# Deformable convolutions: one image's offsets, distances and tents prepared two images ahead, and the tap images' steps set at other places of three engine programs

## The reference, cut to what matters

```
om = conv3x3(xn, w_off) + b_off            # 27 maps: dy, dx of 9 taps, 9 masks
py, px = base + dy, base + dx ; mask = sigmoid(om[18:27])
sampled[k] = bilinear(xn at py[k], px[k]) * mask[k]      # 9 taps
out = einsum('ckhw,ock->ohw', sampled, w)
```

## Time and profile before

| | us |
|---|---|
| median of 3 runs | 1029.12 (1026.18 to 1031.92) |
| the profiled execution | 1027.65 |
| its span, first to last instruction | 1025.9 |
| convolution 0, first offsets to last result | 19.5 to 153 |
| recurrence | 162 to 597 |
| convolution 1 | 608 to 744 |
| busy: PE, DVE, ACT, POOL | 782.2, 547.0, 557.5, 359.9 |

### The profile page before, as it was taken

How to read it: one execution, slowest core, us unless ns; L and a number is a source line. 1 busy time by engine, 2 the same in 40 slices (tenths; PEclk the granted TensorE clock), 3 DMA queues, 4 the chain that set the end, 5 groups by cost and what they waited for, 6 DMA issues and landing times.

```text
span 1025.9 us, 18107 instructions
## 1 busy us (share of the span) xinstructions
PE 782.2 (76%) x6224; PEld 577.1 (56%) x6224; DVE 547.0 (53%) x1560; ACT 557.5 (54%) x1580; POOL 359.9 (35%) x296
## 2 busy tenths in 40 slices
PE   5789886666666666666666467988859999899996
PEld 2476674555555555555555434767736666466664
DVE  3666753555445445333333335666556667567675
ACT  2565653333345455333333335656548888688884
POOL 0646650000000000000000006475528888588884
PEclk8899995555555555555555558999969999899998
DMA  9500000000001100000000000000000010100000
GB/s 221 149 2 1 2 2 1 1 0 1 1 1 73 73 0 1 1 1 1 1 1 0 1 0 1 2 1 2 2 1 2 1 73 2 75 2 1 2 2 22
DMA packets 5861, 18.54 MB, mean 18 GB/s; under 512 B 1093, under 2 KB 2822, under 8 KB 5254
## 3 DMA queue, kind: packets, MB, share of 16 engines
q1 hardware_dynamic: 5478, 17.21, 5.9%
q10 hardware_dynamic: 288, 0.13, 0.1%
HBM read 9.47 MB, written 0.52 MB: 10 GB/s over the span
## 4 chain that ended last, share of the span: by engine, by line
PE 30%; POOL 20%; DVE 18%; ACT 16%; issue 13%; DVEq 1%; POOLq 1%; DMA 0%; SPq 0%; ACTq 0%
POOL zw L806 20%; PE bank L455 9%; DVE bank L1047 6%; PE bank L457 6%; ACT scan_io L702 5%; ACT tcell L706 4%; PE bank L297 4%; DVE hr L1053 4%; PE bank L332 4%; PE bank L349 3%; DVE hid L881 2%; ACT shi L601 2%; PE bank L319 1%; DVE zw L854 1%; DVE flat L846 1%
## 5 line engine op out<-in xcount | busy, mean ns | idle before, releaser
L766 POOL TENSOR_TENSOR st<-tent,tentx 128x768 f32<-128x768 f32 x96 | 140.6, 1500 | 581.1 <-DVE tentx L874 503.4
L806 POOL TENSOR_TENSOR zw<-hid,zw 128x512 f16<-128x512 f32 x176 | 203.9, 1159 | 49.5 <-ACT zw L733 38.8
L455 PE MATMUL bank<-hr,lv 64*64 64x8 f32 x512 | 96.7, 261 | 158.9 <-DVE hr L1053 158.9
L455 PEld LDWEIGHTS bank<-hr,lv 64*64 64x64 f32 x512 | 72.5, 200 | 205.5 <-DVE hr L1053 205.4
L1152 DVE SCALAR_TENSOR_TENSOR hid<-bank,wsc,st 128x512 f32<-128x512 f32 x176 | 132.0, 751 | 75.8 <-ACT st L737 70.4
L702 ACT ACTIVATE scan_io<-bank 64x16 f32<-64x16 f32 x256 | 49.2, 192 | 210.6 <-PE bank L457 210.4
L495 PE MATMUL bank<-st,wh 128*128 128x512 f16 x352 | 137.0, 389 | 11.7 <-POOL st L799 5.4
L1047 DVE TENSOR_TENSOR_SCAN bank<-scan_io 64x32 f32<-64x32 f32 x256 | 57.6, 225 | 163.1 <-ACT scan_io L702 163.1
L737 ACT ACTIVATE st<-bank,wsc 128x512 f32<-128x512 f32 x176 | 121.0, 687 | 35.2 <-PE bank L496 17.5
L881 DVE SCALAR_TENSOR_TENSOR hid<-bank,shi 128x512 f16<-128x512 f32 x144 | 98.1, 690 | 74.0 <-ACT shi L601 72.7
L496 PE MATMUL bank<-st,wl 128*128 128x512 f16 x352 | 136.6, 388 | 0.0
(11 more groups left out here) (149 smaller groups left out, 1135.8 us busy)
## 6 DMA issues: line engine op xcount, KB each, us to landing
w13s<-w SPq DMA_DIRECT2D x8, 704.0 KB, 16.6
w2f<-w SPq DMA_DIRECT2D x4, 384.0 KB, 26.9
w13s<-wh SPq DMA_DIRECT2D x2, 704.0 KB, 3.4
w13s<-wl SPq DMA_DIRECT2D x2, 704.0 KB, 4.6
wh<-w13s SPq DMA_DIRECT2D x2, 704.0 KB, 3.7
wl<-w13s SPq DMA_DIRECT2D x2, 704.0 KB, 5.2
w2f<-w2p SPq DMA_DIRECT2D x2, 384.0 KB, 5.2
w2p<-w2f SPq DMA_DIRECT2D x2, 384.0 KB, 6.0
```

The costliest lines, as they stand in the source:

```text
L455: nc.tensor.matmul(both[:, 0, t, :], lv[:, C:2 * C], prev, start=False, stop=True, skip_group_check=True)
L766: nc.gpsimd.tensor_tensor(st[p][:, t, k:k + KG, :].rearrange("p k (y x) -> p k y x", x=16), ty, tx, ALU.mult)\
L806: nc.gpsimd.tensor_tensor(hl[:, u % MR, :], hid[:, u % MR, :], hh[:, u % MR, :], ALU.subtract)\
```

## The change: what it does

The chain from offsets to tents (PE `offsets`, `turn_offsets`; ACT `offsets`, `turned`, `tents`, `pads`; DVE `distances`, `weighted`) is done for image m + 2 while image m is worked on, where it was done for m + 1. A second set of these steps, for image 1, moves into the part ahead of the loop. Within the loop, ACT `tents` goes from g = 5 to g = 8 and DVE `weighted` from g = 5 to g = 8. Of the tap images, which stay one image ahead, ACT `taps(m + 1, 0)` goes from g = 6 to g = 5, DVE `tap_images(m + 1, 0)` from g = 6 to g = 4, and PE `taps(m + 1, 1)` from g = 8 to behind the last group. No instruction is added or removed, and no wait's condition changes.

```diff
--- before.py
+++ after.py
@@ -369,18 +369,19 @@
                 turn_offsets(0)
                 pe.wait_ge(s(c + "taps"), 2)
                 taps(0, 0)
+                offsets(1, 0)
+                offsets(1, 1)
+                turn_offsets(1)
                 taps(0, 1)
                 for m in range(B):
                     for g in range(NG):
-                        if m + 1 < B:
+                        if m + 2 < B:
                             if g < 2:
-                                offsets(m + 1, g)
+                                offsets(m + 2, g)
                             elif g == 3:
-                                turn_offsets(m + 1)
-                            elif g == 4:
-                                taps(m + 1, 0)
-                            elif g == 8:
-                                taps(m + 1, 1)
+                                turn_offsets(m + 2)
+                        if g == 4 and m + 1 < B:
+                            taps(m + 1, 0)
                         if g == LAG + 2 and m > 0 and m % 2 == 0:
                             turn(m // 2 - 1)
                         turn_weights(m, g)
@@ -388,6 +389,8 @@
                             sums(m, g - LAG)
                         elif m > 0:
                             sums(m - 1, NG - LAG + g)
+                    if m + 1 < B:
+                        taps(m + 1, 1)
                 for h in range(NG - LAG, NG):
                     sums(B - 1, h)
                 turn(BQ - 1)
@@ -632,25 +635,29 @@
                 turned(0)
                 tents(0)
                 taps(0, 0)
+                offsets(1)
+                turned(1)
                 taps(0, 1)
+                tents(1)
+                pads(2)
                 for m in range(B):
                     for g in range(NG):
                         ended = m // 2 - 1 if m % 2 == 0 and m > 0 else None
-                        if m + 1 < B:
+                        if m + 2 < B:
                             if g == 2:
-                                offsets(m + 1)
+                                offsets(m + 2)
                             elif g == 4:
-                                turned(m + 1)
-                            elif g == 5:
-                                tents(m + 1)
-                            elif g == 6:
-                                taps(m + 1, 0)
+                                turned(m + 2)
+                            elif g == 8:
+                                tents(m + 2)
+                        if g == 5 and m + 1 < B:
+                            taps(m + 1, 0)
                         if g == 4 and ended is not None:
                             summed(ended)
                         if g == 7 and ended is not None:
                             result(ended)
-                        if g == 7 and m + 2 < B:
-                            pads(m + 2)
+                        if g == 6 and m + 3 < B:
+                            pads(m + 3)
                         high(m, g)
                     if m + 1 < B:
                         taps(m + 1, 1)
@@ -889,22 +896,23 @@
                 distances(0)
                 weighted(0)
                 tap_images(0, 0)
+                distances(1)
+                flats(1)
                 tap_images(0, 1)
-                flats(1)
+                weighted(1)
                 for m in range(B):
                     for g in range(NG):
                         low(m, g)
                         if g == 0 and m + 2 < B:
                             flats(m + 2)
-                        if m + 1 < B:
-                            if g == 3:
-                                distances(m + 1)
-                            elif g == 5:
-                                weighted(m + 1)
-                            elif g == 6:
-                                tap_images(m + 1, 0)
-                            elif g == 8:
-                                tap_images(m + 1, 1)
+                        if g == 3 and m + 2 < B:
+                            distances(m + 2)
+                        if g == 4 and m + 1 < B:
+                            tap_images(m + 1, 0)
+                        if g == 8 and m + 2 < B:
+                            weighted(m + 2)
+                        if g == 8 and m + 1 < B:
+                            tap_images(m + 1, 1)
 
             def largest():
 
```

## The result

The changed kernel takes 993.68 us (median of 4 runs, 993.37 to 994.94), the kernel before 1028.9 us (4 runs). The ratio is 0.966, 95% interval 0.9636 to 0.9683: 35 us faster. The direction was right, and so was the wait that the change removes; the cost on VectorE that the forecast took off again was not, and the gain was ten microseconds larger than forecast.

The account below looks back on a forecast made before the run. PE was taken as nearly full, with 24.2 us of tap waits in the loops. Seven images at 91.1 us and starts 2.9 us later gained 12.0 and 13.5 us, giving 1003.5 us, range 996 to 1015.

Parts of the forecast that it names:

- the cost on VectorE: In the loops, VectorE instructions slowed beside GpSimd's products; about 7 us taken off the gain.
- The tap wait: PE's tap matmuls L319 idle for VectorE's L854 in the loops; 24.2 us, to be gone entirely.
- The chain given for it: Late in an image: distances, absolute value, tents, groups, tap copies, L854; tents (0.69 + 0.77 us) stand before the copies.
- The clock: PE's lower clock behind waits in the images would be given back; about 8 us, five images by 1.65.
- I take 0.55 us of new ring wait where there is no `turn`: PE waits for low-part banks in the loops: 0.55 us without turn, 0.2 with; bounds 0 and 1.2 each.
- 12.3: Length of image 5 in us: 11.2 on PE, but set by DVE's 11.6 and its ring.
- The cross-check under the sum: Terms of both signs: 24.2 (waits) + about 8 (clock) - 7 (DVE) = 25 us gained.
- Ahead of the loops: Image 1's added set and the wait for pads(2) make T(0, 0) 2.9 us later in each convolution.
- rival 2: No cost on DVE and a fast start, ring waits zero: 996.5 us; chance 0.10.
- Rival 1: DVE becomes the bound, ring waits of 1.2 us and more in each image: 1014.5 us; chance 0.20.
- rival 3: The wait only changes its place, another of the same length appears: 1027 to 1029 us; chance 0.05.
- rival 4: More short waits leave PE at 1.2 GHz, so slower: 1038 us with 35 us at half clock; chance 0.03.

Follow-up runs that it names:

- experiment 1: The kernel before with only TensorE's taps(m + 1, 1) moved behind the last group: 1007.75 us, ratio 0.980.
- experiment 3: The changed kernel with all tap steps put back where they were, offsets, distances and tents staying two images ahead: 1018.12 us, ratio 0.990.
- experiment 4: The changed kernel with only TensorE's taps(m + 1, 1) put back to g = 8: 993.85 us, ratio 0.968.
- experiment 5: The changed kernel with ScalarE's and VectorE's steps for half 0 of the tap images back at g = 6: 1001.02 us, ratio 0.974.
- experiment 7: The changed kernel with ScalarE's pads(2) and VectorE's flats(1) moved earlier ahead of the loops: 989.14 us, ratio 0.963.
- experiment 2: The kernel before with the tap steps at the changed kernel's places, tents and weighted at g = 6, everything one image ahead: 1001.51 us, ratio 0.975.
- experiment 8: The changed kernel with VectorE's distances done twice for images 2 to 7, first into an unread tile: 1022.76 us, ratio 0.995.
- experiment 6: The changed kernel with VectorE's flats(m + 2) moved from g = 0 to g = 8, ahead of weighted: 994.65 us, ratio 0.969.

## Why the prediction was wrong

**The tap wait: right.** It was put at 24.2 us in the loops and gone entirely, and that is what the trace shows. By experiments 1, 3, 4 and 5 it was the order of the tap steps that removed it. The chain given for it was only partly right: with the tents gone from between (experiment 3), 16.8 of the 24.2 us stayed. What mattered was how many groups lie between ScalarE's copies and TensorE's request.

**The clock: right.** It was 1.00 in every window after image 0, and images 1 and 3 lost the 1.65 us that the lower clock had cost. Image 0 has 0.90 in convolution 0 and 0.94 in convolution 1, by the same working 1.4 and 0.8 us, for which the sum had no term.

**The step that failed: "I take 0.55 us of new ring wait where there is no `turn`", and image 5's "12.3".** The two convolutions gained 32.4 us in the profiled executions, forecast 25.5; 4.7 of the 6.9 us between lie in the loops. Images 3 and 5 of convolution 0 are off by 0.75 and 1.3 us; in both PE is busy for the whole window, and new ring wait is nil. The errors of the other images cancel there: images 2, 4 and 6 were 0.3 to 0.35 us shorter than forecast, images 0 and 1 together 1.0 us longer. Some 0.15 to 0.25 us of each of images 2 to 5 is a second, smaller error: PE's own list needs 12.45 and 13.85 us, not the 12.65 and 14.0 that were left when the L319 waits were taken off.

The mechanism of the cost is real. L873 does meet GpSimd and grew to as much as 1.59 us, `flats` was slow in every image, and images 1, at 13.4 us, are near the 13.2 that was forecast. But I charged the same cost to each image. The trace of convolution 0 shows two patterns. In images 1 and 2 GpSimd begins 0.25 and 0.12 us after T(m, 0), and L850 and L873 take some 1.3 and 1.59 us. Image 1 pays for it with 0.9 us. Image 2 has the same delays and pays nothing: with `turn` PE needs 1.4 us more, and VectorE does not, so image 2 runs at PE's pace (13.85). From image 3 on `weighted` ends later after T(m, 0), GpSimd begins 0.74 to 0.79 us after it, L850 takes 0.33 to 0.49 us and L873 0.91 to 0.96, and images 3 to 5 run at PE's pace. Why `weighted` comes later once PE no longer waits for VectorE was not tested. Image 5 is of that kind too: 9.97 us of VectorE in 11.0 us, where I had 11.6. The cross-check under the sum puts 7 us on VectorE; its terms by image add up to 6.1.

**Ahead of the loops: right in kind, too dear.** From the first offsets to T(0, 0) it takes 16.06 us in both convolutions, before 14.05 and 14.4; that is 2.0 and 1.6 us more, forecast 2.9 each. The wait for `pads(2)` is there, 3.0 us, and experiment 7, with `flats(1)` moved as well, shows what it and the order there cost. But `offsets(2, 0)` took 1.81 us, not 2.76: only the last two of its six matmuls were slow, 0.51 and 0.63 us instead of 0.38, and the lower clock fell into image 0 instead.

**The rest of the 35 us.** Stages that the change does not touch differ by 0.4 us in sum (the first norm 1.2 us longer, the experts' part 2 us shorter). The profiled executions differ by 1027.65 - 994.94 = 32.7 us; the medians by 35.2, as the profiled run of before lies 1.3 us below its median and that of after 1.3 us above. I had carried only the first of these over, and a range whose fast end was the middle of rival 2 left no room for such a difference.

**Two images ahead: my reason was not the one.** I priced the earlier tents as a chain that is cut. Experiment 2 shows their main use here once the tap steps are right: GpSimd needs 1.5 us for a product that feeds one and a half groups, 1.0 us a group, where PE has a group each 0.89 us. So it is slower than PE in the groups, and must start well before it; with the old distance it began 1.6 us before T(1, 0) (experiment 2). I had put that at no cost and named it as a cover, but had not seen that the old distance would no longer be enough. The gain of this part is 7.8 us (1001.5 to 993.7), of the tap steps 25.6 us (1027.1 to 1001.5, against the kernel before as it ran beside the experiments). In the convolutions of the traces the shares are 4.8 and 27.5 us.

**Rivals.** Rival 2, with no cost on VectorE, came nearest (996.5). Rival 1 had the right place and not the size: VectorE holds images 0 and 1, and experiment 8 shows that it sets the others too when it has 2 us more to do. Of rival 3 there is little: the ring waits rose from 0.3 to 3.6 us. Of rival 4 there is only the lower clock in image 0.

What stays open: how the gain of experiment 1 is shared. Its rows give 18.2 us of L319 wait, by the windows' clocks some 9 us from the clock, and 4.8 us of new ring waits against them, about 22 us in sum, where the convolutions became 19.9 us shorter; no run separates these. Open is also whether TensorE's step behind the last group costs the changed kernel anything (experiment 4), and no version was tried with `distances` at g = 4 to 6.

## What to carry to other kernels

When two lists meet through a pair of buffers, count the groups of other work between the copy that frees a buffer and the request for it, on both engines; moving either end works, and moving both beyond the need adds nothing. When a cost falls on an engine that is not the bound, do not charge it to each image alike: compare over a full cycle of the loop (here two images), since an image in which the bounding engine has more to do absorbs it (image 2), and look at whether the collision itself comes back at the same moment in the next. And before a step is moved away from a collision, look at who reads its result: four groups of distance between `distances` and the tents were worth more than 0.3 us a time on VectorE.

## What was not expected of the hardware

VectorE's two-input L873 took 0.75 us alone and up to 1.59 us beside GpSimd's products; a second one right behind it took 2.04 us (experiment 8). The delay goes both ways: GpSimd's six products took 9.5 us where they had taken 8.8, and the one that met L873 in image 1 took 2.01 us instead of 1.49. That agrees with the rule named in the prediction (the Trainium skill, SBUF — State Buffer, "Who interferes with whom"): whoever comes second waits. But the price of a collision is set by the moment of arrival, and here that is set by when `weighted` lets GpSimd begin: the same L873 took 0.91 us in image 3 and 1.59 us in image 1. An instruction moved away from the products moved that moment, a later one met them worse, and the total stayed the same (experiment 6); one added cost 2.1 us in the convolutions, nearly three times the 0.75 us that it takes alone (experiment 8).
